# Row maxima in 16 bits and one round, one-pass rounding, and the normalisation on another engine, in a two-layer decoder on one core

## The reference

```python
# three times: attention, softmax over keys
attn = softmax(einsum('bhqd,bhkd->bhqk', q, k) * scale)
# six times: the norm of a row
x = (y - mean(y)) / sqrt(var(y) + 1e-5)
# feed-forward of layer 0
def act_quant(x):
    scale = 127.0 / clip(max(abs(x), axis=-1), 1e-5)
    return clip(round(x * scale), -128, 127) / scale
h = relu(act_quant(x) @ wg.T) ** 2 * (act_quant(x) @ wu.T)
y = x + act_quant(h) @ wd.T
```

## Time and profile before

| | us |
|---|---|
| median of three runs | 1932.95 |
| lowest, highest | 1929.6, 1938.35 |
| the profiled execution's own time | 1935.91 |
| its span, first to last instruction | 1934.1 |
| PE busy | 1605.6 |
| DVE busy | 1247.4 |
| ACT busy | 978.3 |
| POOL busy | 223.3 |
| mean granted clock of PE, as a share of full | 0.92 |

### The profile page before, as it was taken

The page is one execution under the profiler, slowest core; times in us unless marked ns, Lnnn a source line. Parts: engine busy times, 40 slices in busy tenths (PEclk is TensorE's granted clock), DMA queues, the critical chain, the costliest instruction groups (busy, mean ns, idle before and its releaser), DMA issues.

```text
span 1934.1 us, 32136 instructions
## 1 busy us (share of the span) xinstructions
PE 1605.6 (83%) x12626; PEld 1020.7 (53%) x12642; DVE 1247.4 (64%) x2329; ACT 978.3 (51%) x1732; POOL 223.3 (12%) x202
## 2 busy tenths in 40 slices
PE   0568778799899789789989789788989888888878
PEld 0325454466466446365647446365647644546546
DVE  4176686866756776775754966776664777767452
ACT  1146546555464474545465466455456446453633
POOL 2210101001102000111101110110110200101000
PEclk9969899899899899799999898799999988989989
DMA  5440011123201102031220211021320120203020
GB/s 178 117 137 2 1 49 53 53 88 102 80 19 44 55 29 77 9 118 44 86 60 12 88 40 58 20 88 45 107 76 12 55 72 2 77 20 96 26 64 12
DMA packets 116902, 114.91 MB, mean 59 GB/s; under 512 B 10386, under 2 KB 102802, under 8 KB 116754
## 3 DMA queue, kind: packets, MB, share of 16 engines
q1 hardware_dynamic: 116754, 112.85, 19.0%
HBM read 69.04 MB, written 42.99 MB: 58 GB/s over the span
## 4 chain that ended last, share of the span: by engine, by line
PE 62%; DVE 16%; ACT 11%; issue 4%; SPq 3%; DMA 2%; POOL 1%; DVEq 0%; ACTq 0%
PE psum L655 10%; PE psum L755 10%; ACT PB L941 6%; PE psum L874 6%; PE psum L882 6%; DVE nm L1109 6%; PE psum L648 5%; PE psum L739 3%; PE psum L722 3%; PE psum L642 3%; PE psum L766 3%; PE psum L820 2%; PE psum L687 2%; PE psum L832 2%; PE psum L784 2%
## 5 line engine op out<-in xcount | busy, mean ns | idle before, releaser
L1109 DVE TENSOR_REDUCE nm<-psum 128x4 f32<-128x1024 f32 x384 | 451.6, 1217 | 157.2 <-PE psum L722 155.8
L941 ACT ACTIVATE PB<-psum 128x1024 f32<-128x1024 f32 x384 | 382.1, 1024 | 242.2 <-PE psum L755 142.0
L755 PE MATMUL psum<-PB,V 128*32 128x256 f32 x3072 | 238.0, 432 | 19.2 <-ACT PB L941 15.5
L1288 POOL TENSOR_TENSOR XO<-XO,row_b 128x512 f32<-128x512 f32 x80 | 101.7, 1275 | 1306.8 <-ACT XT L913 1306.8
L739 PE MATMUL psum<-QS,KS 50*128 50x256 f16 x1536 | 155.2, 300 | 59.6 <-ACT PB L941 35.9
L722 PE MATMUL psum<-KS,QS 48*128 48x256 f16 x1536 | 148.0, 297 | 57.7 <-DVE nm L1109 14.9
L755 PEld LDWEIGHTS psum<-PB,V 128*32 128x32 f32 x3072 | 90.6, 118 | 105.6 <-issue 53.3
L739 PEld LDWEIGHTS psum<-QS,KS 50*128 50x128 f16 x1536 | 52.5, 98 | 169.3 <-ACT PB L941 65.7
L874 PE MATMUL psum<-XT,W 128*128 128x256 f32 x512 | 128.3, 397 | 3.2 <-ACT XT L913 3.1
L722 PEld LDWEIGHTS psum<-KS,QS 48*128 48x128 f16 x1536 | 56.9, 99 | 138.6 <-issue 34.9
L882 PE MATMUL psum<-W,PB 128*128 128x256 f32 x512 | 117.7, 384 | 0.2 <-ACT PB L1019 0.2
(11 more groups left out here) (159 smaller groups left out, 2668.7 us busy)
## 6 DMA issues: line engine op xcount, KB each, us to landing
heads_dram<-U SPq DMA_DIRECT2D x288, 128.0 KB, 2.0
QS<-heads_dram SPq DMA_DIRECT2D x48, 512.0 KB, 3.5
KS<-heads_dram SPq DMA_DIRECT2D x48, 512.0 KB, 4.3
XO<-in_x SPq DMA_DIRECT2D x16, 256.0 KB, 2.8
Y<-in_ctx SPq DMA_DIRECT2D x16, 256.0 KB, 2.8
out<-XO SPq DMA_DIRECT2D x16, 256.0 KB, 5.0
QS<-GN SPq DMA_DIRECT2D x192, 4.0 KB
W<-in_w SPq DMA_DIRECT2D x2, 1024.0 KB
```

What stands on the lines that cost most here:

```text
L755: ins = pe.matmul(b[SLOT * j:SLOT * j + SLOT, at:at + TOK], value(L, t, PAIRS * e + u, HEADS, HD, SLOT), src, start=(t == 0), stop=(t == T ...
L941: act.activation(PB[L][:, unit % PBUF, :], b[:, 0:1024], ACT.Exp, scale=HD ** -0.5)\
L1109: dve.tensor_reduce(nm[L][:, unit].rearrange("p e t -> p (e t)"), b[:, 0:1024].rearrange("p (a k) -> p a k", a=4), AX.X, ALU.max, negate=T ...
L1288: pool.tensor_tensor(stream(L, it), stream(L, it), row_b[:, occ:occ + 1, :].to_broadcast([P, TT, DIM]), ALU.add).then_inc(xb_ready[L], 1)
```

## The change

The maxima. DVE's reduction writes the negated maximum as one 16-bit number. The cast and the subtraction are gone, and with them DVE's part of negmax. Negmax comes once, after the eighth max; PE turns 16 columns of 8 units and two heads each for both halves of the tokens, ACT copies them once, and SP moves them with two DMAs into one row for each of the two heads, all eight units at once. The exp matmuls have 49 rows, and the first exp waits for the DMAs.

Rounding. Scaling adds 2^23 + 0x6600 (`SHIFT`). The low 16 bits of the result, read as a 16-bit float, are 1536 plus the integer. PE turns every second 16-bit word (`low_half`), and ACT adds -1536 as it copies. The instruction that took the constant off is gone. The rounded h lies in QS for the first half of the tokens and in KS for the second, so DVE's wait for PE's first turning is gone too. In quant one instruction has taken the place of two for the scale and one of the three behind it is gone.

Normalisation. The two instructions of norm are on POOL, in its queue.

The strings `TURNS` and `PLACES` are new as a whole. The core of the diff:

```diff
-    "qk": "pe act dve sp", "stack": "sp", "v": "pe act dve pool", "max": "pe dve", "negmax": "pe dve act sp",
-    "exp": "pe act", "pv": "pe act", "heads": "pe dve", "oT": "pe act", "proj": "pe dve act", "norm": "dve",
+    "qk": "pe act dve sp", "stack": "sp", "v": "pe act dve pool", "max": "pe dve", "negmax": "pe act sp",
+    "exp": "pe act", "pv": "pe act", "heads": "pe dve", "oT": "pe act", "proj": "pe dve act", "norm": "pool",
...
+SHIFT, LOW = 2.0 ** 23 + 0x6600, 1536.0
...
         for u in range(PAIRS):
             add("max", a, u)
-            if u == 5:
-                add("negmax", a, 0)
+        add("negmax", a)
         for u in range(PAIRS):
             add("exp", a, u)
-            if u == 1:
-                add("negmax", a, 1)
...
 TURNS = {
     "pe": (
-        "0011220123303102312000030011110001100200001112200001110011120212101212021102221232120333001222210332"
+        "0020202210133321130001003000222022213000100033000120023203303322231222013223032223302002333321203300"
...
+        def low_half(a):
+            return a.bitcast(F16).rearrange("p (n two) -> p n two", two=2)[:, :, 0]
+
+        def rounded_h(lane, t):
+            return flat2((QS, KS)[t][lane][:, :, :]).bitcast(F32)
...
                 elif name == "negmax":
-                    sp.wait_ge(nmT_ready[L], (it * ATTN + occ) * 2 + unit + 1)
-                    n = PAIRS // 2
+                    sp.wait_ge(nmT_ready[L], it * ATTN + occ + 1)
                     for e in range(2):
-                        sp.dma_start(QS[L][64 * e + 48:64 * e + 50, n * unit:n * unit + n, :], nmT[L][8 * e:8 * e + 8, unit, :])\
-                          .then_inc(nm_row[unit][L], 16)
+                        sp.dma_start(QS[L][64 * e + 48:64 * e + 49, :, :], nmT[L][PAIRS * e:PAIRS * e + PAIRS, :])\
+                          .then_inc(nm_row[L], 16)
...
                 elif name == "exp":
                     b = claim(*step)
-                    if unit in (0, PAIRS // 2):
-                        pe.wait_ge(nm_row[unit // (PAIRS // 2)][L], (it * ATTN + occ) * 32 + 32)
+                    if unit == 0:
+                        pe.wait_ge(nm_row[L], (it * ATTN + occ) * 32 + 32)
...
-                    act.activation(HQT[L][:, :, unit * P:(unit + 1) * P],
-                                   b[:, 0:1024].rearrange("p (i t) -> p i t", t=P), ACT.Copy).then_inc(turned[L], 1)
+                    act.activation(HQT[L][:, :, unit * P:(unit + 1) * P], b[:, 0:1024].rearrange("p (i t) -> p i t", t=P),
+                                   ACT.Identity, bias=shift_c[:, 0:1]).then_inc(turned[L], 1)
...
-                elif name == "negmax":
-                    k, n = it * ATTN + occ, PAIRS // 2
-                    src = nm[L][:, n * unit:n * unit + n].rearrange("p u e t -> p t e u")
-                    dve.wait_ge(max_done[L], k * PAIRS + (unit + 1) * n)
-                    high = own(dve.tensor_copy(nm2[L][:, :, unit, :, 0, :], src))
-                    wait_own(high)
-                    dve.tensor_tensor(nm2[L][:, :, unit, :, 1, :], src, nm2[L][:, :, unit, :, 0, :], ALU.subtract)\
-                       .then_inc(nm_ready[L], 1)
...
-                    n = own(dve.tensor_scalar(H, H, h[:, t, 4:5], MAGIC, ALU.mult, ALU.add))
...
-                    if t:
-                        wait_full(dve, it, "hT", L, 0, 0)
-                    dve.tensor_scalar(HQ[L], H, MAGIC, None, ALU.subtract).then_inc(quantized[L], 1)
+                    wait_own(scaled)
+                    dve.tensor_scalar(rounded_h(L, t), H, h[:, t, 4:5], SHIFT, ALU.mult, ALU.add).then_inc(quantized[L], 1)
...
-                if name == "rope":
+                if name == "norm":
+                    pool.wait_ge(rstd_ready[L], it * NORMS + occ + 1)
+                    for t in range(TT):
+                        pool.tensor_scalar(stream(L, it)[:, t], Y[L][:, t], mv[L][:, t, 0:1], rstd[L][:, t:t + 1],
+                                           ALU.subtract, ALU.mult).then_inc(x_ready[L], 1)
+                elif name == "rope":
```

More of the change, by code:

```diff
@@ L223 @@
+    "2046124167062342301010101067"
 )
@@ L385, in decoder_kernel @@
         part_out, stacked = lane_sem("part_out"), lane_sem("stacked")
-        nm_row = [lane_sem(f"nm_row_{half}") for half in range(2)]
+        nm_row = lane_sem("nm_row")
         turned, hi_ready, values, nmT_ready = (lane_sem(n) for n in ("turned", "hi_ready", "values", "nmT_ready"))
```

205 lines of the change are left out of this document (94 added, 111 removed).

## The result

The changed kernel takes **1938.55 us** (median of 20 runs, 1934.26 to 1946.44), the kernel before 1932.97 us in the 20 runs beside it. The ratio is 1.003 with a 95% interval of 1.0019 to 1.0041: 5.6 us more, inside what the prediction called no change, and half a microsecond above the upper end of its range, 1938. The forecast was 1878. The profiled execution has a span of 1934.3 us, with a mean granted clock of 0.928, against 1934.1 and 0.920 before.

The account below looks back on a forecast made before the run. PE was taken as the bound, busy 1605.6 of 1934.1 us, its idle time many short waits. Against 1935.9 us, -25.6 + 3 + 0 + 8 - 30 - 10 = -54.6 gave 1881, forecast 1878 against the median; range 1838 to 1938.

Parts of the forecast that it names:

- Part 3: Normalisation moved from DVE to POOL: 192 instructions at 640 ns instead of 435, a cost of +8 us.
- DVE relief: DVE loses 153.9 us of work, so PE's idle time falls: -30 us, between 0 and 48.
- clock: With less PE idle time the granted clock rises by 0.0067, making PE's busy time shorter: -10 us.
- the two kinds of stretches: 20 us stretches with DVE busy 80% or more against under 60%: 0.315 us of PE idle per us of DVE.
- Part 1: One round of maxima instead of two: half the transposes' busy and idle time goes, -25.6 us, with +3 as cost.
- The cost of the single round: No exp can start before all eight maxima are turned: 0 to 6 us, taken as +3.
- Part 2: Rounding in one pass, PE turning every second 16-bit word: weight loads cost 0 to 11 us, taken as 0.
- The port: POOL's added instructions can hold DVE up at their shared port: 0 to +10 us, counted at nothing.
- (c): Rival: slower, norms wait in POOL's in-order queue behind other lanes' work; about 1974 us, chance 0.12.
- (a): Rival: PE nearly the only limit, DVE's relief closes no gap; -10 to -25, about 1915 us, chance 0.18.
- (b): Rival: the relief works in full with no costs; -86, about 1847 us, chance 0.15.
- (d): Rival: the new order bunches the lanes' steps, more stretches like 220 to 240 us; about 1928 us, chance 0.08.

Follow-up runs that it names:

- experiment 6: Changed kernel, POOL's norm only multiplying by the inverse root over 256 columns, mean not subtracted: 1897.7 us, ratio 0.981.
- experiment 11: Changed kernel with POOL's norm on 128 of 256 columns, plus 192 DVE instructions of 128x256 that nobody waits for: 1907.5 us, ratio 0.987.
- experiment 3: Kernel before with only 16-bit maxima and one-pass rounding; two rounds of maxima, old order, norm on DVE: 1918.5 us, ratio 0.992.
- experiment 8: Kernel before, old order and two rounds of maxima, with 16-bit maxima, one-pass rounding and POOL's norm on 128 of 256 columns: 1933.4 us, ratio 1.000.
- experiment 10: Changed kernel with POOL's norm on 128 of 256 columns, the maxima's 96 transposes and 48 copies each done twice: 1889.6 us, ratio 0.976.
- experiment 1: Changed kernel with the normalisation back on DVE, every other queue's order kept: 1909.1 us, ratio 0.987.
- the 80 columns: Changed kernel with POOL normalising only the first 80 of 256 columns, waits and orders kept: 1880.2 us, ratio 0.972.
- after: The changed kernel itself, all parts of the change together, against the kernel before: 1938.55 us, ratio 1.003.
- experiment 4: Changed kernel with POOL normalising only the first 128 of 256 columns, waits and orders kept: 1883.8 us, ratio 0.973.
- experiment 9: Changed kernel with the norm split: DVE the first 128 tokens, POOL the second, a semaphore for each half: 1902.0 us, ratio 0.984.
- experiment 7: Changed kernel with the norm on ACT, -mean x root formed first, then root x Y plus that: 1953.3 us, ratio 1.009.

## Why the prediction was wrong

**What bounds the kernel.** Right: PE, with its idle time made of short waits. The idle time did not fall because one source took the place of several: 43.6 us for POOL's norm against 20.5 at the exponential and 10 at the maxima.

**The step that failed is Part 3, the price of a norm on POOL.** The prediction took 640 ns between the fill of 311 and half of a two-input 128x512, and 1.05 us as the far end. The instruction took 1229 ns, beyond that end. The lengths over 80, 128 and 256 columns lie on a line of about 360 ns and 3.4 ns a column. The half of 1275 ns failed for two reasons. Part of an instruction does not shrink with its width: if the 360 ns hold for the addition too, half its width would be about 820 ns (an estimate). And the second step of arithmetic with its scalar per row is another 303 ns (1229 against 926 in experiment 6).
The prediction weighed the GPSIMD Engine Reference of the Trainium skill (4.1, Engine selection), which calls one-input work there roughly line rate. No run here bears that out: the same instruction takes DVE 430 ns and POOL 1229.

**The second failure is how the length was charged.** The prediction had the lanes share the delay, a quarter of it reaching the end. The curve says otherwise: below 0.8 us almost none of it reaches the end, above it 0.55 to 0.7 of the sum over all lanes. Four lanes do not divide a delay here, where PE takes their steps in a written order. A norm that is later than the order allows stops PE for all four, and each lane's norm does so in turn. By the prediction's own working at 1229 ns, 2 x (1229 - 435) x 96 / 4 = 38 us would have come in the place of 10, so the sum would have been 28 us higher, 1906: of the miss of 60 us, 28 are the price and some 33 the sharing. From 640 to 1229 ns the runs give 58 us for 113 us of lane time, 0.52 on average, where the prediction had 0.25.

**With the price as assumed, the sum came out** (1880.2 against 1878), but that is luck in part, since its terms did not all come out:
- *DVE relief, -30, and clock, -10*: right together. They are 40 us for 153.9 of DVE, 0.26 per us; experiment 11 measured 0.31 of the whole time, 23.7 us for 75.4. The slope that the prediction read from the two kinds of stretches, 0.315, is of idle time alone, and its likeness to the 0.31 is chance: the idle time in experiment 11 grew by 0.20 per us of DVE, and busy time, with the clock, gave the rest. In the old order the whole was 0.20 to 0.24 (experiment 3), and nothing in experiment 8. That two of the removed instructions stood in PE's waits was a weak reason to go towards the upper end, since one of the two waits stayed under another name (10.1 us, then 13.0).
- *Part 1, -25.6 + 3*: too large by itself. Transposes and copies are worth some 6 us (experiment 10, which adds no second round of waits), and the whole step from two rounds in the old order to one in the new, these 6 included, is worth 9 us with the norm on DVE (experiments 3 and 1). The prediction had -22.6 for it. For relief, clock and the norm together it had -32, and the runs give -43.3 with the norm at 640 ns (-14.4 in experiment 3 and -28.9 from experiment 1 to the 80 columns): two errors of 11 to 13 us, which cancel. That the waits at the transposes did shrink, 22.1 to 5.0 us, helped only in part: PE then waited elsewhere. The cost of the single round did not show: PE waits for a row of maxima at one exp, 1.1 us.
- *Part 2, 0*: right. The weight load of every second 16-bit word takes 98 to 115 ns, against 112 for the contiguous one, and the turnings of h (L862) are busy 22.6 us in all, before 24.2. ACT's copy with a constant is 0.1 us longer, some 4 us over all 48, on an engine with room.
- *The port, 0*: small. DVE without its norms is busy 1093.6 us in experiment 1 (1168.0 - 74.4) and 1106.9 in after: 13 us, or 4 at 0.31, within the 0 to 10 given. One reading behind it was not exact: the two additions from 501.38 had ended at 505.58, so the subtraction of 505.65 lay beside the bias addition that POOL ran next, not beside them.
- *What was left out*: what the new order is worth for a late norm. The turning of the stream stands five PE steps or fewer behind the last PE step of the part before it in 6 of 64 places, in the old order in 17. Moving the norm to POOL at 0.8 us costs 15 us in the old order and gains 25 in the new, and 50 us lie between experiments 8 and 4. The room behind the norm fits this, but does not show it: PE waits no longer for POOL in experiment 8 (9.9 us) than in experiment 4 (11.9). What causes the 50 us, and how much of it is the single round, is open.

**The account of the result**, from the medians: the 16-bit maxima and one-pass rounding -14.4 (experiment 3), one round and the new order -9.4 (experiment 1), the norm off DVE and on POOL at 0.8 us -25.4 (experiment 4 against 1), and the norm's length beyond 0.8 us +54.8 (after against experiment 4). The sum is the measured 5.6, as it must be, since each step starts where the last ends; in another order the steps are worth something else. Of the 55 us, the profiled spans, which lie 48 apart, have 31 as PE's idle time and 17 as its busy time. The second part goes with the granted clock, 0.928 against 0.937; that the longer waits lower the clock is how it looks (the same matmuls, L755, take 421 ns in after and 413 in experiment 4), and no run holds the one fixed and moves the other.

**The rivals.** (c) named the right engine, and its sign is that of the result by a hair, but the cause it gave is the smaller part. From the starts of the 96 roots and the 96 pairs of norms in the trace, by lane, 24 pairs of after begin more than 0.3 us behind their root, up to 19.9 us, some 175 us in all: POOL's queue does hold norms up. In experiment 4 they are 23 with some 165 us, and that kernel is 55 us faster. Only 10.2 of the 43.5 us of PE's wait are for such norms, so most of that lateness was in places where the order had room. The queue does matter where two norms follow each other, as at 474.92, since the second then pays the longer instruction twice. (c)'s threshold of 2.3 us per norm on a lane's path was not reached either: a norm is 2 x (1229 - 435) = 1.6 us longer, and the loss of 55 us came all the same, because the delays add over lanes. (a) and (b) were not seen. (d) was not seen: at 220 to 240 us PE is busy 16.06 us, not 10.13, and of 92 stretches from 100 us on DVE is busy 80% or more in 11, before in 27.

**The signs named in advance**: the 96 transposes (14.0 us), DVE (1106.9 for 1090), the clock (0.928, in 0.92 to 0.93) and the wait for the row's DMA (1.1 us, under 15) held. PE's busy time (1605.9 for 1580) and its idle time (328.4 for 300) did not. POOL at 457.8 us instead of 350, the norm outside 0.3 to 0.64 us, and "a wait of PE for POOL's normalise of tens of us" named the failure. That last sign was to show (c), the queue, but a long instruction gives it as well. Nor does "if PE's idle does not fall, the relief was the wrong step" hold: it did not fall, and the relief was worth its price all the same (experiment 11).

## What to carry to other kernels

Before a step moves to another engine, time its own form there: same operand kinds, number of arithmetic steps and width, since neither a fill nor half of a wider two-input instruction bounded this one. Where an in-order engine serves several lanes in a written order, hiding can have a threshold: here a latency within the order's slack cost nearly nothing, and one beyond it 0.55 to 0.7 of its sum over all lanes, not a quarter of it. A step that is cheap on one engine and slow on another can be split between both, if each half has its own semaphore (experiment 9). And a load that nobody waits for, put on an engine, prices that engine's relief by itself (experiment 11).

## What the runs showed of the hardware

- POOL's subtract-and-multiply with two scalars per row takes 640, 795 and 1229 ns over 80, 128 and 256 float32 columns, and 926 ns over 256 with the multiply alone. DVE takes 430 to 435 ns for the 256.
- Beside each other, the two norms of experiment 9 took 459 ns on average on DVE instead of 430 and 1273 on POOL instead of 1229. With 192 more instructions on DVE (experiment 11) POOL's norm of 128 columns took 825 ns instead of 795.
- ACT takes 593 ns for 128x256 with a scale and a bias per row and 287 ns for a single column with a scale per row (experiment 7), so nearly half of the time of the wide one does not go by its width. The copy of 1024 PSUM columns went from 1031 ns to 1120 when it got the constant from a tile. The page ScalarE: Activation LUTs of the Trainium skill (What ACT_TABLE_LOAD costs) gives about 93 ns for each operand that points to a column of values; by that rule, the trace agrees, with 89.
- PE loads every second 16-bit word of a tile about as fast as contiguous words: 98 ns (L862 from QS) and 115 (from KS, and L846), before 112 and 102 for the same steps.
